# Two of 128 row tiles in 32 groups of the attention stage fetched row by row by SyncE, and loops with bodies of 32 groups

## What is computed

```python
xh = (x @ W).reshape(-1, H, C)                     # H = 4 heads of C = 32
alpha = leaky_relu((xh[dst] * a_i).sum(-1) + (xh[src] * a_j).sum(-1), 0.2)
ex = exp(alpha - segment_max(alpha, dst)[dst])
out = segment_sum(xh[src] * (ex / segment_sum(ex, dst)[dst])[..., None], dst)
x = layernorm(x + out)
for l in range(3):                                 # h = batch-normalised emb for l > 0
    hk = relu(concat([h[dst], h[src]], 1) @ linA_w[l].T + linA_b[l])
    w = sigmoid(hk @ linB_w[l].T + linB_b[l])
    prop = segment_sum(w * h[src], dst)
    emb = relu(concat([h, prop], 1) @ lin_w[l].T + lin_b[l])
x = layernorm(x + emb @ final_w.T + final_b)
```

## Time and profile before

| | |
|---|---|
| median of 3 runs | 11612.29 us (11603.48 to 11631.4) |
| span of the profiled execution, first to last instruction | 8105.0 us |
| the profiled execution's own time beside the span | none recorded |
| attention stage, first gather to last | 64.4 to 2028.3 us |
| each of three layers | about 2000 us |
| busy: PE, DVE, ACT, POOL | 59%, 60%, 17%, 73% of the span |

### The profile page before, as it was taken

How to read it: one execution, slowest core, us unless ns; L and a number is a source line. 1 busy time by engine, 2 the same in 40 slices (tenths; PEclk the granted TensorE clock), 3 DMA queues, 4 the chain that set the end, 5 groups by cost and what they waited for, 6 DMA issues and landing times.

```text
span 8105.0 us, 161654 instructions
## 1 busy us (share of the span) xinstructions
PE 4794.9 (59%) x26657; PEld 4101.0 (51%) x26658; DVE 4894.9 (60%) x25933; ACT 1394.6 (17%) x5213; POOL 5899.4 (73%) x6246
## 2 busy tenths in 40 slices
PE   6888888888755555555565555555546555555555
PEld 5777777777544444444444444444445444444444
DVE  6777778777655555555555555555555555555555
ACT  3333333333300000000020000000011000000002
POOL 6777777777477777777757777777766777777775
PEclk6555555555655555555565555555556555555555
DMA  5444444444444444444454444444445444444443
GB/s 160 132 132 132 131 131 132 132 131 131 127 134 132 132 132 134 132 132 134 132 154 132 132 132 134 132 132 134 132 116 168 132 132 134 132 132 133 132 132 104
DMA packets 638944, 1078.97 MB, mean 133 GB/s; under 512 B 324360, under 2 KB 399016, under 8 KB 637772
## 3 DMA queue, kind: packets, MB, share of 16 engines
q0 software_dynamic: 296832, 810.95, 34.5%
q1 hardware_dynamic: 306076, 247.79, 10.3%
q10 hardware_dynamic: 35156, 12.72, 0.7%
HBM read 1025.41 MB, written 45.47 MB: 132 GB/s over the span
## 4 chain that ended last, share of the span: by engine, by line
POOL 30%; issue 23%; ACTq 14%; PE 12%; DMA 9%; DVE 7%; ACT 2%; DVEq 2%; POOLq 1%; SPq 0%
POOL G L783 29%; ACTq L1027 10%; DMA G<-mp_rows,idx 5%; PE ps L1816 4%; DMA G<-gat_rows,idx 2%; ACTq L1024 2%; PE ps L1778 2%; ACTq L1026 2%; DMA acc<-in_src 1%; PE ps L1813 1%; PE ps L1805 1%; DVE junk L1605 1%; ACT gate L1018 1%; PE ps L1916 1%; DVEq L1212 1%
## 5 line engine op out<-in xcount | busy, mean ns | idle before, releaser
L783 POOL DMA_INDIRECT G<-mp_rows,idx x4404 | 4165.4, 946 | 1490.4 <-issue 1279.1
L1916 PE MATMUL ps<-selw,G 128*128 128x32 f32 x8808 | 2077.6, 400 | 634.0 <-DVE selw L1614 626.5
L1916 PEld LDWEIGHTS ps<-selw,G 128*128 128x128 f32 x8808 | 1960.5, 328 | 894.9 <-issue 859.3
L1594 DVE TENSOR_TENSOR pen<-ps,G 128x512 f32<-128x512 f32 x1101 | 760.8, 691 | 2476.0 <-DMA G<-mp_rows,idx 2464.2
L1906 PE MATMUL ps<-awin,ring 96*128 96x128 bf16 x4692 | 713.7, 307 | 2160.3 <-DVE ring L1578 2148.0
L783 POOL DMA_INDIRECT G<-gat_rows,idx x1564 | 1488.8, 952 | 491.9 <-issue 442.3
L1906 PEld LDWEIGHTS ps<-awin,ring 96*128 96x128 bf16 x4692 | 413.5, 133 | 2309.3 <-DVE ring L1578 2305.3
L881 ACT COPY idx<-idx_all 128x4 int32 (+1 forms) x1568 | 299.7, 192 | 4716.5 <-issue 4500.7
L1605 DVE SCALAR_TENSOR_TENSOR junk<-pen,ps 128x128 f32<-128x128 f32 x4692 | 1057.2, 278 | 0.1
L1578 DVE TENSOR_TENSOR ring<-ring,ps 96x512 bf16<-96x512 bf16 x1173 | 792.3, 675 | 40.0 <-DMA ring<-rel_dst 40.0
L1816 PE MATMUL ps<-sel,weighted 128*128 128x32 f32 x3128 | 748.9, 404 | 0.0
(11 more groups left out here) (206 smaller groups left out, 5188.7 us busy)
## 6 DMA issues: line engine op xcount, KB each, us to landing
acc<-mp_rows ACTq DMA_DIRECT2D x9216, 1.0 KB
ring<-rel_dst SPq DMA_DIRECT2D x294, 384.0 KB
G<-mp_rows,idx POOLq DMA_INDIRECT x4404
ring<-rel_dst SPq DMA_DIRECT2D x98, 512.0 KB
awin<-mp_dst_rows SPq DMA_DIRECT2D x1173, 24.0 KB
G<-gat_rows,idx POOLq DMA_INDIRECT x1564
mp_rows<-acc SPq DMA_DIRECT2D x36, 512.0 KB, 3.0
mp_dst_rows<-acc SPq DMA_DIRECT2D x36, 384.0 KB, 5.2
```

The costliest lines, as they stand in the source:

```text
L783: pool.indirect_dma_start(out=to[:, t, :], out_offset=None, in_=table, in_offset=bass.IndirectOffsetOnAxis(ap=idx[:, T * u + t:T * u + t + ...
L1594: v.tensor_tensor(pen[:, off % 2, :].rearrange("p (t c) -> p t c", t=T), PS[off % 2][:, :].rearrange("p (t c) -> p t c", t=T), slot(k0, of ...
L1916: i = mm(PS[2 + off % 2][:, 0:W], slot(k0, off)[:, t, 0:D], selw[:, off % 4, W * t:W * t + W], start=(t == 0), stop=(t == T - 1))
```

## The change

The attention stage gets what the layers have, with SP in ACT's part. Its loops on all engines have bodies of 32 groups. Group 21 of each body (`GAT_FAR`, slot 0, in the unused half of `weighted`) and group 5 of each body but the first (`GAT_NEAR`, slot 1, in the unused part of `ring` beside the masks; the tail has it too) get only three gathers from POOL. The last tile's 128 rows come by SP, eight in each step, behind that step's window DMA. SP fetches the row numbers in step 0 and in step 16. `slot`, `lane` and the landing counts now take the stage. To stay within the number of semaphores, the five chained steps `ma hi r1 mid r2` of DVE share one (`tops`), and the four of `al` another; the order of DVE's operations is as before.

```diff
+GAT_FAR = {21: 0}
+GAT_NEAR = {5: 1}
+        gat_lone = [weighted[:, 2:4, :].rearrange("p a c -> p (a c)").rearrange("p (t c) -> p t c", t=T),
+                    ring[:, 4:8, TW:2 * TW]]
+        gat_ids = sb("gat_ids", [1, len(gat_lone) * P], I32)
...
+            def gat_eight_rows(n, part):
+                lo = ROWS * part
+                sp.load(sp_rows, gat_ids[:, P * n + lo:P * n + lo + ROWS])
+                for m, reg in enumerate(sp_rows):
+                    node = sp.snap(reg, min_val=0, max_val=N - 1)
+                    sp.dma_start(gat_lone[n][lo + m:lo + m + 1, T - 1, :], T0[bass.ds(node, 1), :]).then_inc(gat_rows_in[n], 16)
+
+            def gat_fetch_ids(n, k0, at):
+                with nc.allow_non_contiguous_dma(reason="every fourth edge"):
+                    sp.dma_start(gat_ids[:, P * n:P * n + P], lone_sources(k0, at)).then_inc(sp_ids_in, 16)
+
+            def gat_slot_and_ids(k0, off, earlier, ids):
+                if reached(k0, off, V):
+                    sp.wait_ge(gat["R"], k0 + (earlier + 1))
+                    sp.sem_inc(waited, 1)
+                sp.wait_ge(sp_ids_in, k0 + ids)
+                sp.sem_inc(waited, 1)
+
+            def gat_lone_rows(k0, off):
+                if off == 0:
+                    if reached(k0, off, 1):
+                        gat_eight_rows(GAT_NEAR[5], 15)
+                    if not (isinstance(k0, int) and k0 == LAST):
+                        gat_fetch_ids(GAT_FAR[21], k0, 21)
+                elif off <= 16:
+                    if off == 1:
+                        gat_slot_and_ids(k0, off, 21 - V, 16)
+                    gat_eight_rows(GAT_FAR[21], off - 1)
+                    if off == 16:
+                        gat_fetch_ids(GAT_NEAR[5], k0, 5 + V)
+                else:
+                    if off == 17:
+                        gat_slot_and_ids(k0, off, 5, 32)
+                    gat_eight_rows(GAT_NEAR[5], off - 17)
 
-            def gat_body(k0, stop=U):
-                starts = load_starts(k0)
+            def gat_body(k0, stop=V):
                 for off in range(stop):
+                    if off % U == 0:
+                        starts = load_starts(k0, off)
                     if off % 4 == 0:
                         gat_offsets(k0, off)
-                    gat_window(k0, off, starts[off])
+                    gat_window(k0, off, starts[off % U])
+                    if stop == V or off == 0:
+                        if isinstance(k0, int) and k0 == 0 and off == 1:
+                            sp.wait_ge(weightsT_ps, L + 2)
+                        if isinstance(k0, int) and k0 == 0 and off == U:
+                            load_params()
+                        gat_lone_rows(k0, off)
 
             gat_body(0)
-            load_params()
-            with sp.Fori(1, NG // U - 1) as turn:
-                gat_body(turn * U)
+            with sp.Fori(1, BODIES) as turn:
+                gat_body(turn * V)
             gat_body(LAST, REST)
...
+            def gat_gather(k0, off):
+                tiles = T if lane(0, k0, off) is None else T - 1
+                freed = (gat["R"], k0 + (off - U + 1)) if reached(k0, off, U) else None
+                gather(T0, slot(0, k0, off), tiles, off, k0, freed)
```

More of the change, by code:

```diff
@@ L329, in gnn_kernel @@
         act_ids_in = sem("act_ids_in")
+        gat_rows_in = [sem(f"gat_rows_in{n}") for n in range(len(GAT_FAR) + len(GAT_NEAR))]
+        sp_ids_in = sem("sp_ids_in")
         win_in = [sem(f"win_in{n}") for n in range(4)]
@@ L352, in offsets_landed, with lanes, lane, slot @@
             return offs_in[off // 4 % 2], 2 * k0 + (stage * 2 * NG + 16 * (off // U + 1))
[L354 to L362, removed]
-        def gathers_landed(stage, k0, off):
-            if stage == 0 or off % U not in NEAR:
-                return rows_landed(stage, k0, off)
-            earlier = 8 * NG + (stage - 1) * (7 * BODIES * V + 64)
+        def lanes(stage):
+            return (FAR, NEAR) if stage > 0 else (GAT_FAR, GAT_NEAR)
+        def lane(stage, k0, off):
+            far, near = lanes(stage)
+            if off % V in far:
+                return far[off % V]
+            return near.get(off % V) if not (isinstance(k0, int) and k0 == 0) else None
+        def slot(stage, k0, off):
+            n = lane(stage, k0, off)
+            if n is None:
+                return Grows[:, off % U, :, :]
+            return lone[:, n, :, :] if stage > 0 else gat_lone[n]
+        def gathers_landed(stage, k0, off):
+            u = off % U
+            whole, short = 64 * (NG // U - (u == U - 1)), 7 * BODIES * V + 64
+            earlier = sum(short if u in lanes(s)[1] else whole for s in range(stage))
+            if u not in lanes(stage)[1]:
+                return gathered[u], 8 * k0 + (earlier + 64 * (off // U + 1))
             so_far = (0, 48, 112, 160, 224)[off // U + 1] + 16
             if isinstance(k0, int):
-                return gathered[off % U], earlier + so_far + 7 * k0
-            return gathered[off % U], 7 * k0 + (earlier + so_far)
+                return gathered[u], earlier + so_far + 7 * k0
+            return gathered[u], 7 * k0 + (earlier + so_far)
         def single_rows_landed(stage, k0, off):
-            n, l = lane(k0, off), stage - 1
+            n, l = lane(stage, k0, off), stage - 1
+            if stage == 0:
+                return gat_rows_in[n], 64 * k0 + 16 * P * (off % V in GAT_FAR)
             return rows_in[n][l // 2], 64 * k0 + 16 * P * (BODIES * (l % 2) + (off % V in FAR))
@@ L939, in gat_step @@
                     gat_den4(k0, off - 3)
-            for off in range(U):
-                gat_step(0, off)
-            with act.Fori(1, NG // U - 1) as turn:
-                k0 = turn * U
-                for off in range(U):
-                    gat_step(k0, off)
+            for off in range(V):
+                gat_step(0, off, V)
+            with act.Fori(1, BODIES) as turn:
+                for off in range(V):
+                    gat_step(turn * V, off, V)
             for off in range(REST + 3):
@@ L1595, in mp_hidden @@
                                     PS[off % 2][:, :].rearrange("p (t c) -> p t c", t=T),
-                                    slot(k0, off)[:, :, D:2 * D], ALU.add).then_inc(done["hidden"], 1)
+                                    slot(l + 1, k0, off)[:, :, D:2 * D], ALU.add).then_inc(done["hidden"], 1)
                 def mp_logit(k0, off, done=mp):
@@ L1823, in gat_step @@
                         stage(k0, off - lag)
-            for off in range(U):
-                gat_step(0, off)
-            with pe.Fori(1, NG // U - 1) as turn:
-                k0 = turn * U
-                for off in range(U):
-                    gat_step(k0, off)
+            for off in range(V):
+                gat_step(0, off, V)
+            with pe.Fori(1, BODIES) as turn:
+                for off in range(V):
+                    gat_step(turn * V, off, V)
             for off in range(REST + 4):
```

100 lines of the change are left out of this document (48 added, 52 removed).

## The result

The kernel with the change takes 11952.51 us (median, 11951.14 to 11959.84), the kernel before 11611.85 on the same chip: a ratio of 1.0293, 95% interval 1.028 to 1.0305. It is slower by 341 us. The prediction was 11574 (11545 to 11655), faster by 0.33%. It was wrong in sign and far outside its range.

What follows compares the result with a forecast made beforehand. POOL's gathers were taken to bound the attention stage. Removing 24 saves 30.2 us in the profile, with SP's body of 155.7 us under POOL's 158.3; scaled to the median, -38 gives 11574 us (11545 to 11655).

Steps and rivals of the forecast that it cites:

- What bounds the kernel: Attention stage: POOL goes from gather to gather without a real stop, 1.2565 us each; the other engines have slack.
- The gathers removed: Attention: 24 gathers fewer on POOL save 30.2 us; its body falls from 160.8 to 158.3 us.
- The price of eight rows is read from ACT ... I take 3.85: SP's register load and eight row DMAs in each attention step: 3.85 us, bounds 3.6 and 4.15.
- It just fits: SP's attention body, 155.7 us (145.3 to 168.3), stays under POOL's 158.3.
- rest of a step: SP's existing work in each attention step, without the rows: 0.82 us a group.
- turn: Jump back of SP's long attention loop: 2.6 us a turn, bounds 0.2 and 5.6.
- fetches of ids: SP's two fetches of row numbers in each attention body: 1.85 us each, 3.7 a body.
- Turns of DVE as slack: Loop turns of DVE, PE and ACT fall from 48 to 12; removing 36 DVE stalls gains slack, no time.
- The rival of the turns: DVE nearly the pace in timed runs: 36 stalls saved, as much as 202 us, say 11450; chance 0.07.
- From the profiled execution to the median: Span 8105.0 against median 11612.3: the rest spread over the stages, a gather costs 1.43 as much, so -38 us.
- SP as the pace: SP's attention body of 160.8 us or more sets the pace: slower, 11674 at 166, 11702 at 168.3; chance 0.20.

Runs made afterwards that it cites:

- e14: Changed kernel without single rows in attention or layers, POOL gathering all four tiles: ratio 1.0085 to the kernel before, on a chip where that takes 8109 to 8112 us.
- e15: Changed kernel with one reduced group a body (group 21) in place of two: 8092.94 us, ratio 0.9978 to the kernel before.
- e1: The kernel before, unchanged, run and profiled once more: 11783 us, span 11781.4.
- e5: Changed kernel with all of SP's rows issued but read by nobody, POOL gathering all four tiles: ratio 1.0331 to the kernel before.
- e13: Changed kernel run again as it is, on a chip where the kernel before takes 8111.64 us: 8217.41 us, ratio 1.0132.
- e8: Changed kernel with SP issuing four rows a step in place of eight, read by nobody, POOL gathering all four tiles: ratio 1.0003 to the kernel before.
- e10: Changed kernel without single rows anywhere, POOL waiting in attention and layers for the landing of the group before the last: ratio 0.8906 to the kernel before.
- e17: Changed kernel without its single rows in attention, loops of 32 groups kept: ratio 0.9943 to the kernel before.
- e18: Same kernel as e8, run again: ratio 1.0007 to the kernel before.

## Why the prediction was wrong

**What bounds the kernel: right for kind A, wrong for the kernel that was timed.** POOL's gathers are the pace in the profile, and in e14 and e15 too. On kind B they are not: in e1 POOL waits 671.5 us for ACT's copy in 2400, behind the standstills. The prediction used the profile of the one to forecast times of the other.

**The gathers removed: right.** 24 less (1540), and e15 shows that twelve of them are worth 15 us when nothing else is late. On kind B they count too: e5, which issues the same rows and saves no gather, is 0.4% longer than the result, each against its own chip.

**The step that failed first: "The price of eight rows is read from ACT ... I take 3.85", and with it "It just fits".** On kind A, SP's body is 170.8 us and not 155.7, even over the upper bound of 168.3. By terms, from ten bodies of e13 (means):

| term | predicted | measured | error a body, us |
|---|---|---|---|
| block of eight rows, 32 times | 3.85 | 4.15 | 9.8 |
| rest of a step, 32 times | 0.82 | 0.94 | 3.9 |
| turn | 2.6 | 3.3 | 0.7 |
| fetches of ids | 3.7 | 4.4 | 0.7 |

A clean step, 1103.35 to 1108.03 above, takes 4.68 us, as forecast, but it is one of the shorter ones: in the mean a step without turn and fetches is 5.10, and that alone is over POOL's 5.03. The block runs from the start of the register load to the end of the last row; its median is 4.09. The largest error is the load:

```profile
L680 SPq TENSOR_LOAD <-gat_ids x384: 526/717/738, 75.1 to 2114.1; - x192
L683 SPq DMA_DIRECT2D weighted<-gat_rows x1536: 224/228/298, 75.8 to 2034.5; - x192
```

717 ns and not 526. It isn't the tile that makes the difference: the load of the windows' first nodes, the very one of the earlier trace rows, takes 526 in this stage of e14, which has no rows on SP, and 697 in e13:

```profile
L658 SPq TENSOR_LOAD <-per_group x49: 521/526/735, 72.2 to 1986.9; - x49
L658 SPq TENSOR_LOAD <-per_group x49: 691/697/797, 69.2 to 2111.9; - x49
```

And of the loads of ids, the 49 that stand behind another load with no row between take 526 to 545 ns, the 335 behind rows 687 at least. So the price goes with the row DMAs that stand ahead, and ACT's 722, with rows ahead of it, was the nearer row. A row costs SP 228 and not 214 ns, and in 60 of 320 blocks the eight take 3.5 to 3.7 us in place of 3.2 (a tail that a sum of medians leaves out, 0.06 in the mean). The bounds missed because the 0.82, from a loop without rows, and the 3.7 had none. The block, 4.15, lay just on its own bound.

**The turn.** I took 2.6 us. From the last row of a body to the next offsets pass 5.9 in the body above (1085.12 to 1091.02), but that is the slowest of ten jumps back; the others take 3.9 to 5.0, all together 4.5 in the mean. Inside a body the same stretch with its load takes 1.2, so the turn is 3.3. ACT's 2.8 was the near row, and the bound of 5.6 held. The Trainium skill ("Runtime: NRT & Kernel Launch", section "Instruction fetch mechanics") has an engine wait for the fetch behind a taken branch to a page that it no longer holds; the trace agrees in kind, with 2.6 to 4.5 us without an instruction behind SP's ten branches in e13, whose body has 971 instructions, where e14's, of 158, has 0.2. The same section's 200 ns a register is again not what was seen: 717 ns for eight.

**The fetches of ids: nearly right.** In the body above, from the window's issue to the first row pass 2.36 us (1008.18 to 1010.54) where it is 1.3 otherwise, and 0.83 for the fetch: 1.9; in the mean of ten bodies it is 2.2 each. I had 1.85.

**Turns of DVE as slack: right on kind A (5 us), wrong on kind B**, where they give 45 to 65 us. The rival of the turns had the place right and the price three to four times too high.

**From the profiled execution to the median: the step that failed in size.** "Spread over the stages, so that a gather costs 1.43 as much": spread it is, but a gather costs 0.95 us as before. What grew is the time in which the other engines stand, and with it the price of SP's instructions, from 0.42 us a row to 1.25 beside a burst. So the term that I left as it was, SP's step, went from 5.3 (170.8/32, turn and fetches in it) to 8.6 us (275.9/32), against 7.7 for a group: 12 x (275.9 - 32 x 7.7) are 354 us by this estimate. Measured are 341 instead of 106, scaled by no factor of the total.

**The rivals.** SP as the pace, to which I gave 0.20, is the one that came about on both kinds. What would have led to it from the rows at hand: 2.6 us of cover in 158 with a bound of 168 is not "fits"; and no row shows SP loading registers behind single rows.

**What stays open.** What makes a standstill, and why some chips have none. Shown is that they need gathers without a pause, that the work is done but the word of it is late, and that SP's and ACT's instructions slow down then. Which resource they share was not found. Since the experiments' executions all have a recorded span and clock, no run tells a standstill of the chip from one that the recording has a part in. The chip of e8 to e10 was of kind B again 48 minutes later (e17 and e18); over a longer time nothing was tried.

## What to carry to other kernels

Before moving work to an idle engine, sum its whole body with every instruction's own row, tails and turn included, taken where the same instructions stand ahead of it, and make the move only if the upper bound stays under the pace; on kind A half of the rows gained 0.2%, all of them lost 1.3%. When the profile's own time is not the median, find out where the difference lies first: it changed what each engine's instruction costs. A kernel that must run on any such chip does better without single rows issued beside bursts of gathers (0.89 of the time on kind B for 0.9% lost on kind A).

## What the hardware showed beyond that

- The same kernel takes some 8110 us on two chips and 11611 to 11788 us on others, at the same granted clock (0.51 over the span on each kind).
- On the latter, behind four gathers of 128 rows issued 1.25 us apart, PE, DVE and ACT issue nothing for up to 7.7 us (e1), until some 2.8 us after the start of the last gather (median).
- In these stretches SP gets through 17 instructions in 10.1 us, register work as well as DMAs; eight rows take 10 us in place of 3.2. On ACT they take 7.2 in place of 3.1.
- A wait for the landing of each group's gathers takes the standstills away, and makes both kinds equal in this stage (2974 us).
- The same load of eight registers takes 526 ns on SP without row DMAs ahead of it (e14) and 697 with them (e13).
- A jump back costs SP 2.6 to 4.5 us before its next instruction in a loop of 971 instructions (e13), and 0.2 us in one of 158 (e14).
